# Eight key matmuls of a decoder kernel moved from a network's end phase into its four layers

## The chip, the cores and the metric

One core of one Trainium2 chip runs the whole program. The metric is the device time in microseconds (us) of one execution. The engines are PE (TensorE, matrix products and transposes), ACT (ScalarE), DVE (VectorE), POOL (GpSimd) and SP (SyncE, which only issues DMAs here).

## The reference, cut to what matters

Two decoder layers run on eight sequences (b = 0 to 7) of 128 tokens by 512 features, each sublayer followed by a residual sum and a layer norm. Two sublayers meet in the stretch of this case. The first is a small network of depth 4 on 64 channels:

```
h = x @ Win.T + bin
for each of 4 layers:
    y = silu(layernorm(h, ln1w, ln1b))
    y = sconv(y)                       # a long convolution, in the kernel a scan
    h = h + y * scl
    y = layernorm(h, ln2w, ln2b)
    y = silu(y @ W1.T + b1) @ W2.T + b2
    h = h + y
out = layernorm(h, lnlw, lnlb) @ Wout.T + bout
x = layernorm(x + out)
```

The second is cross attention: queries from x, keys and values from the context, which is an input and so is known from the start:

```
q = x @ Wq + bq            # 32 heads of 128
k = ctx @ Wk + bk          # 8 heads of 128
v = ctx @ Wv + bv
x = layernorm(x + softmax(q k^T / sqrt(128)) v @ Wo + bo)
```

## The kernel before, in words

Each engine has its own instruction list in program order; semaphores join them. The order around the change is written out by hand.

**The keys.** K transposed is made for 8 heads (g) and 2 halves of the batch (four sequences, 512 tokens), so in 16 banks' worth of result (n = 0 to 15), each a sum over four blocks of 128 features. This gives 64 matmuls of 128x512 in plain float32, called pieces here; the trace records each as two matmuls (L842). Pieces of even n go to PSUM bank 3, of odd n to bank 7. After the fourth piece of an n, ACT copies the bank to SBUF with the bias (`keys` on ACT, recorded as L1035, "arena<-psum,prm 128x512"). Since the context is ready early, the pieces can stand anywhere before the first scores, and they are used as filling: the table `KV_PLAN` says how many pieces stand at which numbered place, and `kv_pieces(at)` turns it into a range. PE and ACT call `keys(at)` at the same places.

**The places.** 0 is ahead of the layers. In layer l the numbers are 1 + 8l + c: c = 0 and 1 after the transposes of the first norm (L852, one group per half h), c = 2 and 3 after the product that follows the scan (L858), c = 4 and 5 after the transposes of the second norm (L865), c = 6 and 7 after the second product of the feed-forward part (L878, which follows L871). `KV_LAST` = 33 is behind the last norm's transposes (L886), 34 behind the first four output products of the network (`network_out`, L896), and 35 to 38 behind the queries j = 0 to 3 of the first head group.

**The end phase of the network.** PE does `last_turn` (L886), keys, `network_out(0..3)` (L896), keys, `turn_half(0, 0)` and `turn_half(0, 1)` (L914, the transposes of the normed x), `network_out(4, 5)`, `turn_half(0, 2)`, `network_out(6, 7)`, `turn_half(0, 3)`. DVE's list runs beside it: for b = 0 to 3 the sum and statistics (`ln_a`, L1652 to L1656) and the normed x (`ln_b`, L1660), then `x_rest` (L2029, the rest of the split of x into two float32r parts); ACT makes the first part (`turned_half`, "x_split<-psum"). `turn_half(0, 2)` waits for the first `x_rest`, `turn_half(0, 3)` for the second.

**The queries.** `query(0, j)` is 12 matmuls in float32r (L547 to L549) into bank 0. It waits for `q_sb`, that is until ACT has copied the query before out of bank 0 (`query_out`). After `query(0, 3)` the loop over the steps s begins with the scores of step 0 (L982), which wait for the fourth query's copy, for all 16 key copies (`kv_sb`) and for the values.

The lines that put a piece into its place, on PE:

```
        def kv_pieces(at):
            before = sum(c for a, c in KV_PLAN.items() if a < at)
            return range(before, before + KV_PLAN.get(at, 0))
...
            for j in range(GQ):
                query(0, j)
                keys(KV_LAST + 2 + j)
            pe.wait_ge(S.x_sum, lnc(3, B - 1))
            pe.wait_ge(S.kv_sb, 2 * NKV)
```

Of the kernel before, what the change touches and what calls it, by code (L numbers as in the profile page):

```python
# [57 lines left out]

KVL = 8
KV_LAST = 1 + 4 * KVL  # L60
KV_PLAN = {0: 6, KV_LAST: 2, KV_LAST + 1: 4}
for _l in range(4):
    KV_PLAN.update({1 + _l * KVL + 1: 4, 1 + _l * KVL + 2: 2, 1 + _l * KVL + 3: 3, 1 + _l * KVL + 7: 3})
    KV_PLAN[KV_LAST + 2 + _l] = 1
OUT_BANK = (2, 6, 5, 4)
LORA_BANK = (0, 1, 2, 4)
FFN_BANK = (2, 4, 3)
# [78 lines left out]
def decoder_kernel(nc, xT, xtok, ctxT, ctxtok, par, rows, four, win, wx, wdt, wout, qw, sc, ze,  # L146
# [3 lines left out]
    with ExitStack() as ctx:  # L150
# [252 lines left out]
# [5 lines that stand above are left out]
# [1773 lines left out]
```

## Time and profile before

| | us |
|---|---|
| median of 3 runs | 1334.72 |
| lowest and highest of them | 1332.58, 1335.19 |
| the profiled execution | 1333.96 |
| its span, first to last instruction | 1332.2 |
| PE busy in it | 1236.0 (93%) |
| DVE, ACT, POOL busy | 968.5, 748.2, 674.8 |

The span is what the rows of the trace cover; 1.76 us of the profiled execution lie outside it. The stretch of this case is short: the layers run from 674.7 to 777 us of the span, the end phase from there to the first scores at 811.4 us. Layers follow each other every 24.36 us (the first norm's transposes, L852, start at 728.59 us in layer 2 and at 752.95 us in layer 3). In a timeline row the first number is the start, the second the duration of the row's instructions together; a bracket at the end gives the idle time of the engine just ahead and what ended it.

### The profile page before, as it was taken

To read this page: it belongs to the slowest core of one execution; us is meant where nothing else is said; L and a number is where in the kernel's file an instruction comes from. 1 tells how busy PE (TensorE), PEld (TensorE's weight loads), DVE (VectorE), ACT (ScalarE), POOL (GpSimd) and SP (SyncE) were. 2 spreads that over 40 slices of the span, in tenths; PEclk is the share of its full clock that TensorE was granted. 3 is DMA by queue.
4 is the path that set the end of the run, shared out by engine and by line. 5 is a ranking of instruction groups with operands and counts; after the bars stand their busy time and mean duration, and the time that the engine had idled before them with its cause. 6 is when DMAs were issued, how large, how long until landed. Compare 5 with 4: busy or idle time off the path is not lost.

```text
span 1332.2 us, 18653 instructions
## 1 busy us (share of the span) xinstructions
PE 1236.0 (93%) x6464; PEld 925.4 (69%) x6464; DVE 968.5 (73%) x1770; ACT 748.2 (56%) x1478; POOL 674.8 (51%) x535
## 2 busy tenths in 40 slices
PE   6997899999998988998998999999998999999995
PEld 5876677767777764444565547888887888888874
DVE  4785798999999997898657766655554675666676
ACT  5479898989998983332133235544544445444441
POOL 4128988888988870222842126443433543333331
PEclk9999899999999999999999999999998999999999
DMA  6003200122220015002300103222221221111110
GB/s 182 12 26 139 75 25 25 35 93 88 88 72 1 1 56 136 16 9 85 144 9 16 40 24 103 80 73 71 68 75 48 80 79 65 63 64 64 48 48 32
DMA packets 37213, 81.92 MB, mean 61 GB/s; under 512 B 3808, under 2 KB 8160, under 8 KB 35200
## 3 DMA queue, kind: packets, MB, share of 16 engines
q1 hardware_dynamic: 37120, 80.72, 18.5%
q8 instruction: 53, 0.87, 0.3%
q14 instruction: 40, 0.33, 0.1%
HBM read 74.35 MB, written 6.36 MB: 61 GB/s over the span
## 4 chain that ended last, share of the span: by engine, by line
PE 68%; DVE 19%; ACT 6%; issue 5%; POOL 1%; DMA 1%; SPq 1%; DVEq 0%; POOLq 0%; ACTq 0%
PE psum L547 10%; PE psum L549 10%; PE psum L548 10%; PE psum L622 7%; PE psum L636 6%; PE psum L982 4%; DVE arena L1747 4%; PE psum L660 3%; PE psum L647 3%; ACT arena L1035 3%; PE psum L747 2%; PE psum L1001 2%; PE psum L731 1%; DVE lnst L1654 1%; PE psum L871 1%
## 5 line engine op out<-in xcount | busy, mean ns | idle before, releaser
L1471 POOL TENSOR_TENSOR arena<-arena 128x1024 f32<-128x1024 f32 x128 | 300.4, 2370 | 42.7 <-DVE arena L1747 42.5
L1407 POOL TENSOR_TENSOR w_split<-arena,w_split 128x512 fp32r<-128x512 f32 x128 | 168.1, 1333 | 280.3 <-ACT w_split L1035 280.3
L1747 DVE TENSOR_TENSOR_SCAN arena<-psum,arena 128x512 f32<-128x512 f32 x256 | 292.3, 1204 | 15.2 <-ACT psum L1035 15.2
L622 PEld LDWEIGHTS psum<-prm,arena 128*128 128x128 f32 x1024 | 118.7, 142 | 110.3 <-issue 61.8
L1035 ACT ACTIVATE psum<-arena,amat 128x508 f32<-128x508 f32 x256 | 173.3, 709 | 30.4 <-DVE arena L1747 29.4
L622 PE MATMUL psum<-prm,arena 128*128 128x128 f32 x1024 | 148.9, 280 | 38.4 <-DVE arena L1747 34.7
L1035 ACT ACTIVATE arena<-psum,ssmC 128x256 f32<-128x256 f32 x448 | 177.5, 484 | 10.8 <-PE psum L622 10.7
L1035 ACT ACTIVATE arena<-arena 128x512 f32<-128x512 f32 (+2 forms) x86 | 62.8, 734 | 210.1 <-DVE arena L2043 209.1
L1035 ACT ACTIVATE arena<-psum,prm 128x512 f32<-128x512 f32 (+1 forms) x130 | 91.1, 708 | 148.6 <-PE psum L549 70.0
L636 PE MATMUL psum<-prm,arena 128*128 128x128 f32 x1024 | 134.1, 273 | 0.1
L636 PEld LDWEIGHTS psum<-prm,arena 128*128 128x128 f32 x1024 | 117.0, 141 | 0.4 <-ACT arena L1035 0.3
L547 PE MATMUL psum<-x_split,w_split 128*128 128x512 f32 x256 | 106.3, 415 | 2.9 <-DVE x_split L2029 2.8
L1035 ACT ACTIVATE arena<-psum 128x512 f32<-128x512 f32 (+4 forms) x108 | 57.8, 563 | 82.7 <-PE psum L739 33.3
L1391 POOL TENSOR_TENSOR lnrs<-lnve,halfneg 128x1 f32<-128x1 f32 x48 | 28.4, 591 | 143.3 <-DVE lnve L1656 143.3
L549 PE MATMUL psum<-x_split,w_split 128*128 128x512 f32 x256 | 100.9, 394 | 0.0
L548 PE MATMUL psum<-x_split,w_split 128*128 128x512 f32 x256 | 100.8, 394 | 0.0
L547 PE MATMUL psum<-w_split,o_split 128*128 128x512 f32 x256 | 100.7, 394 | 0.0
L549 PE MATMUL psum<-w_split,o_split 128*128 128x512 f32 x256 | 100.1, 391 | 0.0
L548 PE MATMUL psum<-w_split,o_split 128*128 128x512 f32 x256 | 99.6, 389 | 0.0
L2040 DVE TENSOR_REDUCE amax<-psum 128x4 f32<-128x512 f32 x64 | 44.1, 688 | 52.4 <-PE psum L982 52.4
L2059 DVE TENSOR_TENSOR ssmT<-psum,p_split 128x512 fp32r<-128x512 f32 x64 | 44.2, 691 | 51.5 <-ACT p_split L1035 51.4
L2049 DVE TENSOR_REDUCE asum<-arena 128x4 f32<-128x512 f32 x64 | 43.9, 686 | 44.0 <-ACT arena L1035 44.0
(230 smaller groups left out, 2544.0 us busy)
## 6 DMA issues: line engine op xcount, KB each, us to landing
arena<-wq SPq DMA_DIRECT2D x64, 256.0 KB, 2.6
arena<-wo SPq DMA_DIRECT2D x64, 256.0 KB, 2.8
arena<-bc_scratch SPq DMA_DIRECT2D x8, 1024.0 KB, 5.2
arena<-win SPq DMA_DIRECT2D x16, 256.0 KB, 2.7
v_keep<-row SPq DMA_DIRECT2D x16, 256.0 KB, 2.1
arena<-v_keep SPq DMA_DIRECT2D x1, 4096.0 KB, 12.8
arena<-xT SPq DMA_DIRECT2D x8, 256.0 KB, 5.5
x_tok<-wv SPq DMA_DIRECT2D x1, 2048.0 KB, 7.7
```

The costliest lines, as they stand in the source:

```text
L547: mm(o, l[0], r[0], start=start, stop=False)
L548: mm(o, l[0], r[1], start=False, stop=False)
L549: return mm(o, l[1], r[0], start=False, stop=stop)
L622: last = nc.tensor.transpose(hT[:, c, b % 2, e, :], hst[:, (2 * k + e) % 4, b * L:(b + 1) * L], ident)
L636: last = mm(bank[6 + e][:, b * L:(b + 1) * L], hTs[:, k % 2, b, e, :], ident, start=(n == 0 and b == 0), stop=(n == NS - 1 and b == HB - 1 ...
L982: last = mm(bank[1][:, j * P:(j + 1) * P], qT[:, v % 2, j, b * L:(b + 1) * L], KT[:, v % NKV, gb * L:(gb + 1) * L], start=True, stop=True)
L1035: return nc.scalar.activation(o, i, f, **k)
L1407: gp.tensor_tensor(out_, whole, hi.bitcast(F32), ALU.subtract).then_inc(done, 1)
L1471: gp.tensor_tensor(bu[:, i % 4, :, :], dtu[:, (2 * j + e) % 4, :].unsqueeze(1).to_broadcast([P, NG, HT]), Brep[:, q * NG:(q + 1) * NG, :], ...
L1747: v.tensor_tensor_scan(hst[:, i % 4, :], decay_bank(i), bu[:, (k // NG * 2 + e) % 4, k % NG, :], 0.0, ALU.mult, ALU.add).then_inc(S.scan_d ...
L2040: link(v.tensor_reduce(amax[:, :], ps, AX.X, ALU.max))
L2059: v.tensor_tensor(p_lo[:, r % 2, :], bank[2][:, :], p_hi[:, r % 2, :].bitcast(F32), ALU.subtract).then_inc(S.p_rest, 1)
```

## The change

Only the table changes. Each layer gets four pieces instead of three at c = 3 and at c = 7, so eight more in all; the four pieces at place 34 and the four at places 35 to 38 are gone, the two at 33 stay.

```diff
-KV_PLAN = {0: 6, KV_LAST: 2, KV_LAST + 1: 4}
+KV_PLAN = {0: 6, KV_LAST: 2}
...
-    KV_PLAN.update({1 + _l * KVL + 1: 4, 1 + _l * KVL + 2: 2, 1 + _l * KVL + 3: 3, 1 + _l * KVL + 7: 3})
-    KV_PLAN[KV_LAST + 2 + _l] = 1
+    KV_PLAN.update({1 + _l * KVL + 1: 4, 1 + _l * KVL + 2: 2, 1 + _l * KVL + 3: 4, 1 + _l * KVL + 7: 4})
```

The file is one line shorter, so every line number behind the table is one lower after it. On PE, from the product behind the scan of layer 2 to the transposes of layer 3's first norm, the order before is this (here a piece counts once):

```order
L858 MATMUL psum<-arena 128x64 x4
L842 MATMUL psum<-arena 128x512 x3
L865 MATMUL psum<-prm,arena 64x128 x8
L871 MATMUL psum<-arena 128x512 x4
L878 MATMUL psum<-arena 128x64 x16
L842 MATMUL psum<-arena 128x512 x3
L852 MATMUL psum<-prm,arena 128x128 x8
```

and after the change:

```order
L857 MATMUL psum<-arena 128x64 x4
L841 MATMUL psum<-arena 128x512 x4
L864 MATMUL psum<-prm,arena 64x128 x8
L870 MATMUL psum<-arena 128x512 x4
L877 MATMUL psum<-arena 128x64 x16
L841 MATMUL psum<-arena 128x512 x4
L851 MATMUL psum<-prm,arena 128x128 x8
```

One piece has come in ahead of each norm's transposes; the other three layers read alike.

On PE in the end phase, from the last norm's transposes to the first half's last transposes, before:

```order
L886 MATMUL psum<-prm,arena 64x128 x8
L842 MATMUL psum<-arena 128x512 x2
L896 MATMUL psum<-dwout_sb,arena 128x512 x4
L842 MATMUL psum<-arena 128x512 x4
L914 MATMUL psum<-prm,x_tok 128x128 x8
L896 MATMUL psum<-dwout_sb,arena 128x512 x2
L914 MATMUL psum<-prm,x_tok 128x128 x4
L896 MATMUL psum<-dwout_sb,arena 128x512 x2
L914 MATMUL psum<-prm,x_tok 128x128 x4
```

and after:

```order
L885 MATMUL psum<-prm,arena 64x128 x8
L841 MATMUL psum<-arena 128x512 x2
L895 MATMUL psum<-dwout_sb,arena 128x512 x4
L913 MATMUL psum<-prm,x_tok 128x128 x8
L895 MATMUL psum<-dwout_sb,arena 128x512 x2
L913 MATMUL psum<-prm,x_tok 128x128 x4
L895 MATMUL psum<-dwout_sb,arena 128x512 x2
L913 MATMUL psum<-prm,x_tok 128x128 x4
```

The four pieces between the output products and the transposes are gone; behind these rows the one piece after each of the four queries is gone too.

The copies on ACT move with the fourth pieces. Before, each layer had one at c = 1, c = 2 and c = 7, and two followed in the queries' stretch or just ahead of it. After, layers 0 and 2 have one at c = 1, 2, 3 and 7, layers 1 and 3 one at c = 1, 3 and 7, and the last stands at place 33. In layers 0 and 2 the one at c = 3 stands on ACT directly ahead of the two copies of the second norm (L1034 after the change, d_tr), as ACT's list of layer 2 shows, before:

```order
L1035 ACTIVATE arena<-psum,prm 128x512 [waits kv_ps] x2
L1035 ACTIVATE arena<-psum,prm 64x512 [waits d_tr] x2
L1035 ACTIVATE arena<-psum,prm 128x512 [waits d_f1]
```

and after:

```order
L1034 ACTIVATE arena<-psum,prm 128x512 [waits kv_ps] x3
L1034 ACTIVATE arena<-psum,prm 64x512 [waits d_tr] x2
L1034 ACTIVATE arena<-psum,prm 128x512 [waits d_f1]
```

A third key copy now stands ahead of the second norm's copies.

## Rows read from the trace of the kernel before

**Rows 1.** The page: shares of the span by engine in the chain that ended last.
```profile
PE 68%; DVE 19%; ACT 6%; issue 5%; POOL 1%; DMA 1%; SPq 1%; DVEq 0%; POOLq 0%; ACTq 0%
```

**Rows 2.** Timeline of PE in layer 2: start, duration, line, shape, count, idle before.
```profile
729.95 3.60 PE L842 MATMUL psum<-arena 128*128 128x512 f32 x8
733.38 1.00 PE L858 MATMUL psum<-arena 128*128 128x64 f32 x8
...
736.89 2.79 PE L842 MATMUL psum<-arena 128*128 128x512 f32 x6
740.36 0.63 PE L865 MATMUL psum<-prm,arena 128*64 128x128 f32 x4 [0.68 <-DVE arena L1974]
741.23 0.63 PE L865 MATMUL psum<-prm,arena 128*64 128x128 f32 x4 [0.24 <-DVE arena L1974]
741.86 3.70 PE L871 MATMUL psum<-arena 64*128 64x512 f32 x8
...
749.11 2.79 PE L842 MATMUL psum<-arena 128*128 128x512 f32 x6
752.95 0.66 PE L852 MATMUL psum<-prm,arena 128*128 128x128 f32 x4 [1.05 <-DVE arena L1974]
```

**Rows 3.** Timeline of ACT at layer 2's second norm.
```profile
741.03 0.78 ACT L1035 ACTIVATE arena<-psum,prm 64x512 f32<-64x512 f32 x1 [4.15 <-PE psum L865]
```

**Rows 4.** Waits, 676 to 780 us: who for whom, us in total, times, longest.
```profile
PEld psum L871 <- ACT arena L1035: 1.1, 4, 0.3
```

**Rows 5.** Timeline of PE in the end phase.
```profile
783.73 3.70 PE L842 MATMUL psum<-arena 128*128 128x512 f32 x8
787.27 1.04 PE L914 MATMUL psum<-prm,x_tok 128*128 128x128 f32 x8
788.24 1.98 PE L896 MATMUL psum<-dwout_sb,arena 64*128 64x512 f32 x4
790.40 0.63 PE L914 MATMUL psum<-prm,x_tok 128*128 128x128 f32 x4 [0.19 <-DVE x_split L2029]
...
794.94 0.50 PE L547 MATMUL psum<-x_split,w_split 128*128 128x512 f32 x1 [1.41 <-DVE x_split L2029]
...
798.83 0.47 PE L547 MATMUL psum<-x_split,w_split 128*128 128x512 f32 x1
...
806.51 0.47 PE L547 MATMUL psum<-x_split,w_split 128*128 128x512 f32 x1
...
811.40 1.13 PE L982 MATMUL psum<-arena 128*128 128x128 f32 x8 [1.06 <-ACT arena L1035]
```

**Rows 6.** Timeline of DVE in the end phase.
```profile
781.26 0.69 DVE L1652 TENSOR_TENSOR x_tok<-x_tok,psum 128x512 f32<-128x512 f32 x1 [3.49 <-PE psum L896]
...
784.75 0.54 DVE L1660 TENSOR_SCALAR x_tok<-x_tok,lnmv,lnrs 128x512 f32<-128x512 f32 x1
...
786.94 0.54 DVE L1660 TENSOR_SCALAR x_tok<-x_tok,lnmv,lnrs 128x512 f32<-128x512 f32 x1
...
789.57 0.68 DVE L2029 TENSOR_TENSOR x_split<-psum,x_split 128x512 fp32r<-128x512 f32 x1
```

**Rows 7.** Timeline of ACT between the queries.
```profile
798.00 0.69 ACT L1035 ACTIVATE arena<-psum,prm 128x512 f32<-128x512 f32 x1 [3.84 <-PE psum L549]
...
810.62 0.68 ACT L1035 ACTIVATE arena<-psum,prm 128x512 f32<-128x512 f32 x1
```

**Rows 8.** Stretches: length, busy us and count of PE, PEld, DVE, ACT, POOL, PEclk, DMA.
```profile
609.60:613.00 3.40, 0.69 (x5) 0.52 (x5) 3.30 (x7) 1.99 (x4) 0.00 (x0) 1.00 0.00 0
613.00:616.40 3.40, 3.40 (x4) 1.33 (x5) 1.60 (x4) 0.00 (x0) 1.48 (x7) 0.50 0.00 0
1011.60:1015.70 4.10, 1.50 (x13) 1.12 (x12) 2.64 (x4) 1.63 (x4) 0.00 (x0) 1.00 0.21 64
1015.90:1022.50 6.60, 5.19 (x15) 3.82 (x14) 2.15 (x4) 0.96 (x2) 0.00 (x0) 0.50 0.00 0
783.80:788.20 4.40, 4.40 (x17) 2.31 (x16) 4.19 (x11) 0.73 (x2) 1.56 (x2) 1.00 0.00 0
```

## The prediction

> **What bounds the kernel now.** I read the page first: of the span's 1332.2 us the chain of work that ended last is two thirds PE, one fifth DVE [rows 1]. That is an average. The change lives in 137 us of it, so the timelines of that stretch decide, engine beside engine.
>
> In a layer the chain changes hands. PE runs without a gap from the second norm's transposes through both feed-forward products into the key pieces, and then waits for DVE's norm. The timeline of PE in layer 2 shows the two waits at which the change puts work [rows 2]: the pieces from 736.89 end 0.68 us before the transposes L865 may start, and those from 749.11 end 1.05 us before L852. Both were ended by DVE (L1974), which had no earlier moment. So PE is not late there, it is filled up to a remainder. The other layers repeat the pattern with their period of 24.36 us.
>
> In the end phase the bound is DVE. It starts its first sum at 781.26 and reaches the first `x_rest` (L2029) at 789.57 [rows 6], and in 783.80 to 788.20 it is busy 4.19 of 4.40 us [rows 8]. Its whole list in that time hangs on nothing that PE does late. PE's third group of transposes (L914 at 790.40) waits for that `x_rest` and starts 0.15 us after its end at 790.25 [rows 5, 6]. Then come two output products, the fourth transposes, ACT, DVE and the first query at 794.94.
>
> From the first query on, PE and ACT alternate: a query, its copy out of bank 0 by ACT, and beside the copy one key piece.
>
> **What the move costs in the layers.** One piece at c = 3. Four pieces take 733.38 - 729.95 = 3.43 us from their start to the next instruction's start [rows 2], so from 736.89 they would reach 740.32. L865 starts at 740.36. It fits, by 0.04 us. Cost 0, at the least; at the most, if all four layers miss by a little, 0.1 each.
>
> One piece at c = 7: 749.11 + 3.43 = 752.54, and L852 starts at 752.95 [rows 2]. It fits by 0.4 us. The cover is PE's wait for DVE. Without this cover a piece costs its own 0.86 us (3.43 / 4), and eight of them 6.9 us.
>
> The copies on ACT. They number 16 as before, but in layers 0 and 2 one now stands at c = 3, directly ahead of the copy of the second norm. Its bank is full when the fourth piece ends, at 740.32 + 0.16 (rows of four pieces last 3.60 and free PE after 3.43) = 740.48. Each key copy takes 0.69 us [rows 7], so ACT is free at about 741.1 to 741.2. Before, ACT began the norm's copy at 741.03 [rows 3]. The first product behind it, L871, does wait for this copy: its weight load waited four times for ACT, 0.3 us at the longest [rows 4], and 741.03 + 0.78 = 741.81 meets its start at 741.86 [rows 2, 3]. So the delay of 0.1 to 0.2 us goes straight onto the path, since PE is gapless behind it. In two layers that is 0.15 x 2 = 0.3 us; from 0 to 0.5. The copy at c = 7 of those layers begins about 752.7 and is over at 753.4, while L852's result comes at 752.95 + 0.66 = 753.6: nothing.
>
> The weights of the keys. SP loads head g's weights once the piece count frees the buffer. The pieces now come earlier, but so does the release, as both follow the same counter, and a load lies at least one group of layers' places (over 10 us) ahead of its use. Nothing is queued on SP behind it that could start earlier, because the query weights wait for the last layer's product. Cost 0.
>
> **What it brings in the end phase.** The four pieces at place 34 lasted from 783.73 to 787.27, 3.54 us of PE [rows 5]. Without them the first transposes could start when x of b = 0 is normed, 784.75 + 0.54 = 785.29, and the second when b = 1 is, at 787.48 [rows 6]. That is 2.0 and 0.3 us sooner. But what follows needs `x_rest`, and DVE reaches it in its own order at 789.57 whatever ACT and PE did. The third transposes still start at 790.40 and the first query at 794.94. Of 3.54 us nothing is won; PE stands idle instead. From both sides: 0, or if DVE had waited for ACT, which its busy time excludes, some tenths. I take 0.
>
> The four pieces behind the queries. A query and its piece take 798.83 - 794.94 = 3.89 us [rows 5]. Without the piece the next query waits for ACT: from a query's start to ACT's start 798.00 - 794.94 = 3.06, the copy 0.69 [rows 7], and from a copy's end to PE's start 811.40 - (810.62 + 0.68) = 0.10 [rows 5, 7]. Together 3.85. The piece was hidden behind the copy: 0.04 us won on the first, between 0 and 0.1 on each of the next two. Say 0.1 for the three.
>
> The last piece is different. Before, the scores at 811.40 waited for ACT's copy of the last keys, begun at 810.62 after the last piece [rows 5, 7]. After, that copy is long done, and the scores need only the last query's copy. The last query began at 806.51 [rows 5]; 806.51 + 3.85 = 810.36, less the 0.1 above 810.26. Won: 811.40 - 810.26 = 1.1 us with that 0.1. Its bounds are 0.9 (a first matmul slower after a gap) and 1.4.
>
> **The sum.** -1.1 + 0.3 = -0.8 us against the profiled execution's 1333.96, which lies 0.76 under the median of 1334.72. The same steps taken from the median: 1334.72 - 0.8 = 1333.9 us. The bounds of the terms give -1.4 to 0. Behind 811.40 all engines' lists shift together, and from there PE is the bound, so I carry the gain to the end unchanged.
>
> **The rivals.** First, the clock, and with it a slower kernel. After the change PE between 783.8 and 788.2 has only two short groups of transposes, about 1.1 us together, with idle times of some 1.5 us ahead of each (785.3 - 783.8, and 787.5 less 785.9); before, it was busy throughout [rows 8]. The trace shows what emptier stretches do: in 609.60 to 613.00 PE was busy 0.69 us, and then it ran at 1.2 GHz (granted 0.50) for 3.4 us; after 1011.60 to 1015.70 with 1.50 us busy came 6.6 us at 1.2 GHz [rows 8]. If the clock falls at about 787.1, the output products at 788.24 (1.98 us for four records [rows 5]) are at half speed. With 3.4 us of it, the third transposes start some 0.8 us later; with 6.6 us, both pairs of products (1.7 us each more, less the part that meets the full clock again) and the transposes are hit, about 2.3 us. Net of the 0.8: 1333.9 + 0.8 = 1334.7 to 1333.9 + 2.3 = 1336.2 us. If the low clock reaches the first query too, its 3.06 us [rows 5, 7] become up to 6, and the time 1339. It decides as soon as the loss passes 0.8. For it: the new gap is nearly as empty as the two that fell. Against: it is two gaps with work between, not one of 2.6, and the queries' new gaps of 0.8 us are no more than those that the layers have at full clock. A quarter.
>
> The Trainium skill (TensorE: Matmul & The Clock Gate, Part 4: PE-mode transpose) says that transposes don't count as work for the clock in the way matmuls do. By that rule all of 783.8 to 788.2 is one idle stretch, and the fall would be near certain, for a time of about 1336.2 in place of 1333.9. Both stretches of [rows 8] that ended in a fall held transposes and the rule fits them, but they had little work of any kind, so they don't show it.
>
> Second, the layers miss their turn. The fit at c = 3 is 0.04 us. If the pieces or the copies push L865, L871 and DVE by 0.3 us in every layer, the gain of 1.1 is given back: 1334.8, and at 0.5 each 1335.6. Against it: the second half's transposes have another 0.24 us of wait [rows 2], which takes up a late first half. One in eight.
>
> Third, a larger gain: the removed PE time counts in full, 3.54 + 4 x 1.0 = 7.5 us (a piece among queries is 3.89 less the query's 3.06 - 0.16 = 2.9), less the 0.3, so 1327.5. This needs DVE and ACT to be faster than their rows. One in twenty.
>
> **How the numbers follow.** My forecast, 1333.9 with 1333.1 to 1334.7 as its own range, has 0.57; the clock 0.25; the layers 0.13; the larger gain 0.05. Each comes with the spread of a median of a few runs (before: 1332.58 to 1335.19). The range 1332.0 to 1336.3 leaves out the larger gain and the clock's worst, and some of the spread. About 0.2%, 2.7 us, is what a measurement of this kernel can tell from no change. Faster by more (under 1332.0): the larger gain and a little of the forecast's spread, 0.09. Slower by more (over 1337.4): the clock's worst and the spread above its 1336.2, 0.07. Within: 0.84.
>
> **What would show it.** Right: in the timeline of PE the first query starts within 0.3 us of the distance it had from the first DVE sum (794.94 - 781.26 = 13.7); queries 3.8 us apart with 0.8 us idle "<-ACT" between; scores 15.3 us after the first query instead of 16.5; the layers' period 24.36 in layers 1 and 3, up to 24.6 in 0 and 2; no idle ahead of the first L865 and about 0.2 ahead of L852. Wrong: a granted clock under 1 between 785 and 800 us, products of L896 at double length, or layer periods above 24.7.

## The result and the profile after

The changed kernel takes 1342.62 us (median of 6 executions, 1339.75 to 1350.37), the kernel before 1334.45 us (6 executions, 1332.58 to 1335.19): a ratio of 1.0067 with an interval of 1.004 to 1.0095. It is slower. Measured once more, 12 executions beside 35 of the kernel before (e12 below), it is 1341.66 against 1335.92 us, ratio 1.0035, interval 1.0014 to 1.0056. (The ratios here and below are not the quotients of the two medians and can differ from them by 0.1%.) Single executions lie up to 8 us (changed) and 11 us (before) over their medians, with a lower mean clock; hence the wide intervals.

The page of the changed kernel, its span and its row of granted clocks (40 slices of 33.5 us, in tenths of 2.4 GHz):

```profile
span 1339.9 us, 18653 instructions
PEclk8999899999999999999999979999998999999999
```

The slice at 7, the 24th (770 to 804 us), is the end phase. In the kernel before it stood at full clock.

The timeline of PE in layer 2 answers to [rows 2] (all line numbers behind the table are one lower):

```profile
738.67 3.65 PE L841 MATMUL psum<-arena 128*128 128x512 f32 x8
742.16 0.61 PE L864 MATMUL psum<-prm,arena 128*64 128x128 f32 x4
743.00 0.63 PE L864 MATMUL psum<-prm,arena 128*64 128x128 f32 x4 [0.24 <-DVE arena L1973]
743.76 3.70 PE L870 MATMUL psum<-arena 64*128 64x512 f32 x8
...
751.01 3.65 PE L841 MATMUL psum<-arena 128*128 128x512 f32 x8
754.85 0.66 PE L851 MATMUL psum<-prm,arena 128*128 128x128 f32 x4 [0.18 <-DVE arena L1973]
```

Both groups of pieces have grown by one, the wait ahead of the first L864 is gone, and that ahead of L851 has shrunk from 1.05 to 0.18 us. From the start of the first L864 to that of L870 it is 1.60 us; before it was 1.50. It is 1.60 us in layer 0 too, and 1.47 us in layers 1 and 3, where the key copy at this place follows the second piece and not the fourth. So the 0.1 us is the copy on ACT, which now stands ahead of the norm's; the waits of the layers, 1.1 us before [rows 4], have grown with it.

```profile
PEld psum L870 <- ACT arena L1034: 1.3, 4, 0.4
```

The end phase on PE, as [rows 5]:

```profile
782.02 3.70 PE L895 MATMUL psum<-dwout_sb,arena 64*128 64x512 f32 x8
787.27 0.66 PE L913 MATMUL psum<-prm,x_tok 128*128 128x128 f32 x4 [1.54 <-DVE x_tok L1659]
789.45 1.12 PE L913 MATMUL psum<-prm,x_tok 128*128 128x128 f32 x4 [1.52 <-DVE x_tok L1659]
790.49 3.77 PE L895 MATMUL psum<-dwout_sb,arena 64*128 64x512 f32 x4
794.20 1.11 PE L913 MATMUL psum<-prm,x_tok 128*128 128x128 f32 x4
795.24 3.78 PE L895 MATMUL psum<-dwout_sb,arena 64*128 64x512 f32 x4
798.95 1.11 PE L913 MATMUL psum<-prm,x_tok 128*128 128x128 f32 x4
...
801.48 0.79 PE L546 MATMUL psum<-x_split,w_split 128*128 128x512 f32 x1 [1.41 <-DVE x_split L2028]
...
807.33 0.47 PE L546 MATMUL psum<-x_split,w_split 128*128 128x512 f32 x1 [0.87 <-ACT arena L1034]
...
818.85 1.13 PE L981 MATMUL psum<-arena 128*128 128x128 f32 x8 [0.87 <-ACT arena L1034]
```

Two waits of 1.5 us stand where the four pieces were. From the second transposes on, PE's work takes nearly twice its time: four transposes 1.1 instead of 0.6 us, two output products 3.8 instead of 2.0. The two stretches show why, with the granted clock third from the end:

```profile
785.60:788.80 3.20, 0.78 (x5) 0.42 (x4) 2.99 (x9) 0.60 (x1) 0.82 (x2) 0.98 0.00 0
788.80:805.80 17.00, 14.94 (x30) 7.92 (x31) 9.88 (x22) 1.79 (x3) 2.09 (x3) 0.50 0.00 0
```

TensorE was busy 0.78 of 3.20 us and then ran at 1.2 GHz for 17.0 us. And DVE's list, which continues [rows 6], now has long waits. The third and fourth `x_rest` before:

```profile
791.69 0.69 DVE L2029 TENSOR_TENSOR x_split<-psum,x_split 128x512 fp32r<-128x512 f32 x1 [0.38 <-ACT x_split L1035]
794.19 0.69 DVE L2029 TENSOR_TENSOR x_split<-psum,x_split 128x512 fp32r<-128x512 f32 x1 [1.81 <-ACT x_split L1035]
```

and the first, third and fourth after:

```profile
791.49 0.68 DVE L2028 TENSOR_TENSOR x_split<-psum,x_split 128x512 fp32r<-128x512 f32 x1
...
795.98 0.69 DVE L2028 TENSOR_TENSOR x_split<-psum,x_split 128x512 fp32r<-128x512 f32 x1 [2.75 <-ACT x_split L1034]
800.73 0.69 DVE L2028 TENSOR_TENSOR x_split<-psum,x_split 128x512 fp32r<-128x512 f32 x1 [4.06 <-ACT x_split L1034]
```

The first `x_rest` still comes where DVE's own list puts it, 8.31 us after its first sum (783.18; before 789.57 - 781.26 = 8.31). The third and fourth wait for ACT, which waits for PE's transposes. These waits were 0.38 and 1.81 us and are 2.75 and 4.06 us; together they have grown by 4.62 us, and that is by how much more the first query is late.

Where the 7.7 us between the two spans went, by the starts of the same instructions:

| stretch | before | after | difference |
|---|---|---|---|
| to the first key pieces | 674.68 | 676.33 | +1.65 |
| layers, to the first output product | 105.42 | 105.69 | +0.27 |
| from there to the first query | 14.84 | 19.46 | +4.62 |
| first query to the second | 3.89 | 5.85 | +1.96 |
| second query to the scores | 12.57 | 11.52 | -1.05 |
| scores to the end of the span | 520.8 | 521.05 | +0.25 |

The first row is not the change's. No instruction moved ahead of 676 us; there this execution had 3.4 us at 1.2 GHz near 471 us (granted clock 0.89 over 465 to 480 us, 1.00 in the one of before). The 0.25 us of the last row I leave open. The four rows between add up to 5.8 us, which is the change's part; the medians of e12 lie 5.7 us apart.

### The profile page after: what moved, and what is told of

Read it like the earlier page. It is cut to its first block, busy times and chain, and to the rows that moved or that the text cites. A ratio compares the mean times of both kernels' runs of the same rounds, so it can differ in the third digit from the quotient of the medians.

```text
span 1339.9 us, 18653 instructions
## 1 busy us (share of the span) xinstructions
PE 1243.6 (93%) x6464; PEld 929.6 (69%) x6464; DVE 968.9 (72%) x1770; ACT 748.6 (56%) x1478; POOL 675.4 (50%) x535
## 4 chain that ended last, share of the span: by engine, by line
PE 68%; DVE 18%; ACT 6%; issue 4%; POOL 1%; DMA 1%; SPq 1%; DVEq 0%; POOLq 0%; ACTq 0%
PE psum L546 10%; PE psum L548 10%; PE psum L547 10%; PE psum L621 7%; PE psum L635 6%; PE psum L981 4%; DVE arena L1746 4%; PE psum L659 3%; ACT arena L1034 3%; PE psum L646 3%; PE psum L746 2%; PE psum L841 2%; PE psum L1000 2%; DVE lnst L1653 1%; PE psum L870 1%
## 5 line engine op out<-in xcount | busy, mean ns | idle before, releaser
L1034 ACT ACTIVATE psum<-arena,amat 128x508 f32<-128x508 f32 x256 | 173.1, 708 | 29.8 <-DVE arena L1746 28.9
L1034 ACT ACTIVATE arena<-psum,ssmC 128x256 f32<-128x256 f32 x448 | 177.8, 484 | 11.6 <-PE psum L621 11.6
L1034 ACT ACTIVATE arena<-arena 128x512 f32<-128x512 f32 (+2 forms) x86 | 62.8, 734 | 209.9 <-DVE arena L2042 208.9
L1034 ACT ACTIVATE arena<-psum,prm 128x512 f32<-128x512 f32 (+1 forms) x130 | 91.0, 709 | 144.7 <-PE psum L548 73.6
L1034 ACT ACTIVATE arena<-psum 128x512 f32<-128x512 f32 (+4 forms) x108 | 57.8, 563 | 82.7 <-PE psum L738 33.3
```

Source lines behind the costliest of these rows:

```text
L1034: return nc.scalar.activation(o, i, f, **k)
```

## The experiments

My theory after the result: emptying the place ahead of the transposes lets TensorE's clock fall, and all of the loss is what the end phase then takes longer. Rivals: the new waits between the queries do it or share in it; the pieces in the layers cost more than they seem to. For each kernel the table gives the time from the first output product (L895) to the first scores (L981) in its profile, besides the whole. The time to the scores leaves out what differs elsewhere between executions. The kernel before ran beside each group.

| kernel | product to scores, us | low clock there, us | median (executions), us | median of before, us | ratio (interval) |
|---|---|---|---|---|---|
| before | 31.30 | none | | | |
| changed | 36.83 | 788.8 to 805.8 | 1342.62 (6) | 1334.45 | 1.0067 (1.004, 1.0095) |
| e1 | 30.24 | none | 1334.94 (12) | 1336.34 | 0.9999 (0.9974, 1.0024) |
| e2 | 38.44 | 793.0 to 813.5 | 1343.08 (7) | 1336.34 | 1.0044 (1.003, 1.0058) |
| e3 | 30.27 | none | 1335.91 (12) | 1336.34 | 1.0003 (0.9984, 1.0023) |
| e4 | 30.25 | none | 1335.29 (11) | 1336.34 | 0.9992 (0.9983, 1.0001) |
| e5 | 30.35 | none | 1335.10 (12) | 1335.88 | 0.9987 (0.9965, 1.0009) |
| e6 | 30.27 | none | 1335.49 (12) | 1335.88 | 0.9989 (0.9963, 1.0015) |
| e7 | 28.53 | none | 1332.84 (12) | 1335.88 | 0.9976 (0.9951, 1.0002) |
| e8 | 30.76 | 793.2 to 796.6 | 1333.83 (12) | 1335.88 | 0.9975 (0.9953, 0.9996) |
| e9 | 30.28 | none | 1336.07 (12) | 1335.92 | 1.0007 (0.9982, 1.0033) |
| e10 | 30.49 | 787.2 to 790.6 | 1335.57 (9) | 1335.92 | 1.0004 (0.9978, 1.0031) |
| e11 | 28.07 | none | 1332.84 (12) | 1335.92 | 0.9989 (0.9963, 1.0015) |
| e12 | 36.97 | 793.0 to 810.1 | 1341.66 (12) | 1335.92 | 1.0035 (1.0014, 1.0056) |

### e1 and e2: each half of the change alone

```diff
# e1: the pieces behind the queries moved, those ahead of the transposes kept
+KV_PLAN = {0: 6, KV_LAST: 2, KV_LAST + 1: 4}
...
+    KV_PLAN.update({1 + _l * KVL + 1: 4, 1 + _l * KVL + 2: 2, 1 + _l * KVL + 3: 3, 1 + _l * KVL + 7: 4})
# e2: the pieces ahead of the transposes moved, those behind the queries kept
+KV_PLAN = {0: 6, KV_LAST: 2}
...
+    KV_PLAN.update({1 + _l * KVL + 1: 4, 1 + _l * KVL + 2: 2, 1 + _l * KVL + 3: 3, 1 + _l * KVL + 7: 4})
+    KV_PLAN[KV_LAST + 2 + _l] = 1
```

> Only the four pieces behind the queries are moved (into the layers, one more at c = 7 of each); the four between the network's output products and the transposes stay. Theory A (the emptied stretch before the transposes lets the clock fall, and that is the whole loss): the clock stays at 2.4 GHz from 675 to 1012 us, queries 3.84 us apart with about 0.87 us idle, scores about 1.1 us sooner: 0.5 to 1.5 us faster than before. Theory B (the new waits between the queries are part of what keeps the clock low): a low clock between 795 and 812 us and a loss of 2 us or more.

> Only the four pieces ahead of the transposes are moved (one more at c = 7 of each layer); those behind the queries stay. Theory A: the clock falls near 788 us as in the changed kernel, the first query starts 18 to 20 us after the first output product instead of 14.8, 5 to 8 us slower than before. Theory B, in which the queries' waits are needed too: a short fall at most, 0 to 2 us slower.

PE's timeline of e1 from the transposes on:

```profile
795.50 0.50 PE L546 MATMUL psum<-x_split,w_split 128*128 128x512 f32 x1 [1.41 <-DVE x_split L2028]
799.38 0.47 PE L546 MATMUL psum<-x_split,w_split 128*128 128x512 f32 x1 [0.87 <-ACT arena L1034]
...
810.90 1.13 PE L981 MATMUL psum<-arena 128*128 128x128 f32 x8 [0.87 <-ACT arena L1034]
```

The waits between the queries are there, 0.87 us each, the queries are 3.88 and 3.84 us apart as with pieces between them, and the scores come 30.24 us after the first product, 1.06 sooner than before. The stretch from 785 to 800 us has full clock:

```profile
785.00:800.00 15.00, 12.53 (x46) 6.82 (x46) 12.31 (x28) 4.07 (x7) 3.03 (x5) 1.00 0.00 0
```

e2 has no such waits and falls, for 20.5 us:

```profile
788.15 3.70 PE L896 MATMUL psum<-dwout_sb,arena 64*128 64x512 f32 x8
793.39 1.12 PE L914 MATMUL psum<-prm,x_tok 128*128 128x128 f32 x4 [1.54 <-DVE x_tok L1660]
...
796.62 3.78 PE L896 MATMUL psum<-dwout_sb,arena 64*128 64x512 f32 x4
...
807.61 0.80 PE L547 MATMUL psum<-x_split,w_split 128*128 128x512 f32 x1 [1.41 <-DVE x_split L2029]
...
826.59 1.13 PE L982 MATMUL psum<-arena 128*128 128x128 f32 x8 [1.06 <-ACT arena L1035]
```

```profile
790.00:795.00 5.00, 2.97 (x9) 1.25 (x7) 4.69 (x14) 0.46 (x1) 1.33 (x2) 0.80 0.18 52
```

So the queries' waits are out as a cause, and the loss belongs to the four pieces ahead of the transposes. The gain of 1.06 us shows in the trace alone: over whole executions e1 can't be told from before.

e2 shows one thing more. Its first group of transposes already runs at half speed (1.12 us), and a granted clock of 0.80 over 790 to 795 us puts the fall at 793.0, only 1.1 us into the first wait and directly behind 3.7 us of output products without a rest. So the fall does not need both waits. Nor does the share of busy time order the cases by itself: in the 3.40 us ahead of this fall the products filled 2.25, more than in the stretches of [rows 8] that ended in one. They were products over 64 rows. Whether that is the reason, or at what moment the wait came, no run here settles.

### e3, e4 and e9: the empty place filled again, with three kinds of work

In the changed kernel, work that nobody reads is put where the four pieces were. It goes to PSUM bank 3, behind the last copy out of it.

```diff
# e3: four products over 128 rows
+            def fill(n):
+                for i in range(n):
+                    mm(bank[3][:, :], wk_sb[:, 0, 0:P], ctxT_sb[:, 1, i % KD, :], start=True, stop=True)
...
-            keys(KV_LAST + 1)
+            pe.wait_ge(S.kv_sb, 15)
+            fill(4)
# e4: in place of fill(4), 32 transposes
+            for i in range(32):
+                nc.tensor.transpose(bank[3][:, i % 4 * P:(i % 4 + 1) * P], ctxT_sb[:, 0, i // 4 % KD, i % 4 * P:(i % 4 + 1) * P], ident)
# e9: fill(4) with products over 64 rows
+                    mm(bank[3][:, :], wk_sb[0:DIM, 0, 0:P], ctxT_sb[0:DIM, 1, i % KD, :], start=True, stop=True)
```

> The changed kernel with four needless 128x512 float32 matmuls (their result is never read) in the place that the four moved pieces left ahead of the transposes. Theory A: no fall there, 0.5 to 1.5 us faster than before, some 8 us faster than the changed kernel. A rival in which the loss comes from moved work in the layers or from another order of the copies: it stays 5 to 8 us slower.

> The changed kernel with 32 needless 128x128 transposes (about 3.5 us of the engine) in the same place. If any work of TensorE keeps its clock: as with the matmuls, 0.5 to 1.5 us faster than before. If transposes don't count as work, as the Trainium skill says (TensorE: Matmul & The Clock Gate, Part 4: PE-mode transpose): the clock falls and it is 5 to 8 us slower than before.

> As e3, four needless products ahead of the transposes in the changed kernel, but over 64 rows in place of 128, of the same length in time. If the rows a product fills matter to the clock, and 64 are too few to keep it: it falls, and the time is 5 to 8 us over that of before. If they keep it like 128 rows and like transposes: as e3, within 1 us of before. In between (some executions fall) the theory that only the share of busy time counts is out as well.

The filling and its stretch in e4, and then in e9:

```profile
783.85 3.72 PE L906 MATMUL psum<-prm,arena 128*128 128x128 f32 x32
783.80:788.20 4.40, 4.40 (x41) 4.35 (x40) 4.18 (x11) 0.16 (x1) 1.59 (x3) 1.00 0.00 0
```

```profile
784.44 3.59 PE L906 MATMUL psum<-arena 64*128 64x512 f32 x8
780.90:789.00 8.10, 8.10 (x26) 3.79 (x25) 6.59 (x16) 1.03 (x2) 3.13 (x4) 1.00 0.10 32
```

All three keep the clock, and product to scores is 30.27, 30.25 and 30.28 us: the same to 0.03. With the place filled, the whole loss is gone and the scores' gain of 1.0 us is there. Over whole executions all three are level with the kernel before; the 0.5 to 1.5 us that I had expected to see there are too small for it. The pieces in the layers are the changed kernel's in all three, so they don't carry the loss. The rule of the Trainium skill (TensorE: Matmul & The Clock Gate, Part 4: PE-mode transpose) that transposes don't count as work is not borne out here for keeping the clock: in e4 the engine did nothing but float32 transposes for 3.7 us, and more of them behind, with a granted clock of 1.00, and none of its 11 executions took over 1337.24 us. Whether transposes alone can lift a clock that is down, no run here shows. Products over 64 rows, 7.1 us of them without a rest in e9, kept the clock too: the first half of e9's expectation fell.

### e5: the layers' part by itself

As e3, and one needless product behind each query too, so that TensorE does all that it did before and eight pieces more.

```diff
+            fill(4)
...
                 query(0, j)
-                keys(KV_LAST + 2 + j)
+                fill(1)
```

> The changed kernel with needless 128x512 float32 matmuls in all eight places that the moved pieces left (four ahead of the transposes, one behind each query). TensorE so does what it did before, and eight pieces more in the layers: this times the layers' part alone. If the layers take the pieces in their waits: 0 to 0.5 us slower than before, and the layers of the trace 0.3 us longer in all. If they don't: 2 us slower or more. Against the kernel with four needless matmuls (e3) it gives back the 1 us that the freed scores brought.

The queries and the scores:

```profile
797.22 0.50 PE L546 MATMUL psum<-x_split,w_split 128*128 128x512 f32 x1 [1.41 <-DVE x_split L2034]
...
812.73 1.13 PE L987 MATMUL psum<-arena 128*128 128x128 f32 x8
```

The layers are as in the changed kernel (100.41 us from the transposes of the first norm of layer 0 to the first output product, 100.43 there), and the whole is 1335.10 us against 1335.88, interval 0.9965 to 1.0009: no cost that can be measured. My last expectation missed. I wrote that the products behind the queries would give back the 1 us. They don't (30.35 us, against 30.27): what had delayed the scores was not the last piece on PE but ACT's copy of the last keys, and a needless product has none.

### e6: half of the filling

```diff
+KV_PLAN = {0: 6, KV_LAST: 2, KV_LAST + 1: 2}
...
+    KV_PLAN.update({1 + _l * KVL + 1: 4, 1 + _l * KVL + 2: 2, 1 + _l * KVL + 3: 3 + _l % 2, 1 + _l * KVL + 7: 4})
```

> The changed kernel, but two of the four pieces stay ahead of the transposes (two layers take one piece less at c = 3). TensorE's empty stretch there shrinks from two waits of 1.5 us to about one. If the clock falls as soon as any such wait is there: 5 to 8 us slower than before. If half the filling is enough: 0.5 to 1.5 us faster. A mixture over the executions (some near the one time, some near the other) would say that it hangs on where in the chip's own rhythm the stretch lies.

```profile
785.41 1.98 PE L841 MATMUL psum<-arena 128*128 128x512 f32 x4
787.23 0.60 PE L913 MATMUL psum<-prm,x_tok 128*128 128x128 f32 x4
789.20 0.66 PE L913 MATMUL psum<-prm,x_tok 128*128 128x128 f32 x4 [1.37 <-DVE x_tok L1659]
```

One wait of 1.37 us is left, and the clock stays up. One of its 12 executions took 1346.64 us, the other eleven at most 1337.67; the kernel before had such single ones as well (up to 1346.96), so a mixture doesn't show. Two pieces were enough in this one profile.

### e8, e10 and e12: why it stayed low so long

In the changed kernel TensorE never rested from 789.45 to 800.06 us, and still ran at 1.2 GHz to 805.8. Most of that time it did the output products, which use 64 of the array's 128 rows. In e8 they are taken over 128 rows; the added rows of the weights are zero, so the result is the same.

```diff
+        dwout_all = dwout_rows[:, :]
...
+            link(gp.memset(dwout_rows[DIM:P, :], 0.0))
...
-                mm(bank[OUT_BANK[b % HB]][:, :], dys[0:DIM, b // HB, (b % HB) * L:(b % HB + 1) * L], dwout_sb,
+                mm(bank[OUT_BANK[b % HB]][:, :], dys[:, b // HB, (b % HB) * L:(b % HB + 1) * L], dwout_all,
```

> The changed kernel, with the network's output products (L895) over 128 rows in place of 64; the added rows of the weights are zero, so the result is the same, and so is a product's duration. In the changed kernel the clock stayed at 1.2 GHz through 10.6 us in which TensorE never rested, most of it in these products, and came back only in the first query. If half-filled products don't lift the clock: with full rows it comes back before the first query, at 792 to 799 us in place of 805.8, and the loss shrinks from 8 to 2 to 5 us. If rows don't matter: as the changed kernel, low to the first query.

> The kernel of e8 once more, for a second profile: its 12 executions had a median of 1333.8 us and the profiled one 1339.4, the slowest. If full rows in the output products keep the clock in most executions: a profile with no fall between 785 and 800 us, the scores 30 to 30.5 us after the first output product, and 1332 to 1334.5 us. If it falls in all and only comes back sooner: a fall of 3.4 us near 790 again and 1336 us or more.

> The changed kernel itself, on the chip and beside the executions of before that the other three use. If it falls in every execution: every time 5 us or more over the median of before, and a profile with a low clock for 13 us or more from about 789 us.

PE's timeline of e8:

```profile
793.21 1.11 PE L914 MATMUL psum<-prm,x_tok 128*128 128x128 f32 x4 [1.52 <-DVE x_tok L1661]
794.12 3.12 PE L896 MATMUL psum<-dwout_sb,arena 128*128 128x512 f32 x4
797.08 0.60 PE L914 MATMUL psum<-prm,x_tok 128*128 128x128 f32 x4
797.51 1.88 PE L896 MATMUL psum<-dwout_sb,arena 128*128 128x512 f32 x4
```

The fall is there, but the clock is back after 3.4 us, within the first pair of products. The second pair takes 1.88 us, and product to scores is 30.76 us instead of 36.83. Of the loss, of which I had expected 2 to 5 us to stay, nothing is left: e8 is even below the kernel before by its interval, though e10, the same kernel, is level with it. e10's profile gives the same picture with other times; its stretch at the low clock:

```profile
787.20:790.60 3.40, 2.98 (x7) 1.89 (x8) 3.30 (x8) 0.60 (x1) 1.54 (x2) 0.52 0.00 0
```

Of the two outcomes written down for e10 the profile decides for the second: the full rows don't prevent the fall, they end it. (Its time, 1335.57 us, lies just under the 1336 that I had put to it.) e12, the changed kernel again, has its 17.1 us at 1.2 GHz:

```profile
793.00:810.20 17.20, 15.24 (x31) 8.13 (x32) 10.04 (x23) 1.79 (x3) 2.08 (x3) 0.50 0.00 0
```

Its 12 executions range from 1338.90 to 1349.07; the lowest is 3.0 us over the median of before, not 5 as I had written, though none is below it. So two things make the loss: the empty place, in which the clock fell in all five profiles that have it (changed, e2, e8, e10, e12), and the 64-row products behind it, through which it stayed down until the queries. The second rests on one edit, the rows, with two profiles on one side and three on the other.

### e7 and e11: a version with a shorter end phase

e7 starts from e1 and lets the third and fourth transposes write banks of their own, 7 and 3, ahead of the last two output products, so that they need no `x_rest`; they wait for the last two key copies instead, and ACT and DVE read the new banks (these waits and reads are not in the lines shown). e11 has the full rows of e8 as well.

```diff
-            turn_half(0, 2, 0)
+            turn_half(0, 2, 7)
+            turn_half(0, 3, 3)
             for b in range(HB + 2, B):
                 network_out(b)
-            turn_half(0, 3, 1)
```

> The pieces as in e1 (four kept ahead of the transposes, none between the queries), and the third and fourth transposes write PSUM banks of their own (7 and 3, in which the keys are done) in place of 0 and 1, ahead of the last two output products; so they no longer wait for DVE's rests. If DVE's list is the bound of this stretch, as I said, it now runs on without its waits for ACT (0.4 and 1.8 us): the first query 1.3 to 2.2 us sooner, and 2 to 3.5 us faster than before in all. If something else binds there: as e1.

> e7 (four pieces kept ahead of the transposes, none between the queries, own banks for the third and fourth transposes) with the output products over 128 rows. If both gains stand beside each other: the scores 28.5 us after the first output product as in e7, and 2 to 4 us faster than before. The rows should add nothing where the clock doesn't fall.

PE and then DVE in e7:

```profile
792.30 1.27 PE L915 MATMUL psum<-prm,x_tok 128*128 128x128 f32 x8
793.50 1.98 PE L895 MATMUL psum<-dwout_sb,arena 64*128 64x512 f32 x4
795.41 0.50 PE L546 MATMUL psum<-x_split,w_split 128*128 128x512 f32 x1
```

```profile
793.62 1.30 DVE L2030 TENSOR_TENSOR x_split<-psum,x_split 128x512 fp32r<-128x512 f32 x2 [0.17 <-ACT x_split L1036]
```

DVE waits 0.17 us for ACT where it had waited 0.4 and 1.8, and the first query comes without a wait, 13.15 us after the first output product instead of 14.84. With the scores' gain, product to scores is 28.53 us, 2.8 less than before. e11 has 28.07, and there I missed: I had written that the rows add nothing where the clock holds. Four output products over 128 rows take PE 3.44 us to the next instruction, over 64 rows 3.62, and in e7 PE is what the first query follows. The medians are 3.0 and 3.1 us under those of before, but both intervals hold 1: the gain is shown in one profile each and not settled over executions.

## Why the prediction was wrong, point by point

**The layers: right.** I had 0.3 us in all, from ACT's copy in layers 0 and 2, and nothing for PE. The trace has 0.27 us. L870 starts 1.60 us after the first L864 in layers 0 and 2, 0.10 more than before, and not later than before in layers 1 and 3. The pieces fit at c = 3 with nothing over and leave 0.18 us ahead of L851, where I had 0.04 and about 0.2. e5 finds no cost over executions.

**The end phase: the mechanism of the forecast was right, while the clock held.** The first `x_rest` comes 8.31 us after DVE's first sum in both kernels; nothing was won by emptying PE. In e3, e4 and e9, which hold the clock, the stretch is what the forecast said: 1.0 us less, all of it the last copy of the keys. But DVE is the bound only as far as the first `x_rest`. Behind it it waited, before the change too, 0.38 and 1.81 us for ACT and so for PE's transposes: from 790.4 us on PE's speed counts directly, and there the low clock struck.

**The queries: right.** They follow each other 3.84 us apart with 0.87 us of wait for ACT, and from the second one to the scores it is 1.05 us less; I had 1.1.

**The clock: here it failed.** The sum has no term for it; it stands only in the first rival, and two steps of that were wrong. The first was its chance. I gave it a quarter and argued that two gaps with work between are less than one of 2.6 us. My rows said nothing for that: one stretch of them that ended in a fall had 0.69 us busy in 3.40, and the new one, which I had called "nearly as empty", has 0.78 in 3.20. In all five profiles with this place empty the clock fell, in e2 within the first of the two gaps. The second was its length, and so its price. I took 3.4 or 6.6 us from [rows 8]; it was 17.0 us. The cost was 4.62 us to the first query and 1.96 us in it, together 6.6, where I had 0.8 to 2.3 and, beyond it, a first query doubled as an afterthought, for 1339 us at the most. I had priced the low clock as if the work behind the gap would lift it. e8 and e10 show what I had missed. The work behind the gap is 64-row products; made over 128 rows, the clock comes back after 3.4 us and 6.1 to 6.3 of the 6.6 us are gone. A fall of 3.4 us, which I had priced at 0.8 us, costs at least 0.5 in e8 and 0.2 in e10 (30.76 and 30.49 against e3's 30.27); the full rows gain something of their own, 0.46 us in e11 against e7, so the price may be up to that much higher.

**A slip in the sum.** The bounds of the terms, -1.4 to 0, give 1333.3 to 1334.7 from the median; the forecast's own range says 1333.1. It changes nothing here.

**The rule of the Trainium skill** (TensorE: Matmul & The Clock Gate, Part 4: PE-mode transpose) pointed to the outcome that came, but its reason is not the one at work: transposes alone kept the clock in e4, and in e2 it fell before any transpose had run in the place.

## What to carry to other kernels

Before work is taken out of a place in which the engine waits anyway, read how empty the place becomes and what stands ahead of it and behind it: here the filling cost nothing, and without it TensorE ran at 1.2 GHz for 17 us. Price a fall of the clock by the work that follows, not by the shortest fall in the trace. A chain that is bound by another engine can be shortened where that engine waits (e7: banks of their own for two transposes), and not by giving the idle engine less to do.

## What the runs showed of the hardware that I had not expected

- Products over 64 rows kept a full clock (e9, 3.6 us of filling behind 3.7 us of output products, granted 1.00), yet TensorE stayed at 1.2 GHz through 10.6 us of such products and transposes without a rest. With the same products over 128 rows it was back at 2.4 GHz after 3.4 us, in two profiles.
- Thirty-two transposes in a row, 3.7 us, kept the clock as well as products did.
- The zeros in the added rows did not matter to this: half of what the 128-row products multiply is zero, and the clock came back all the same (e8, e10).
- One wait was enough: in e2 the clock fell 1.1 us after the end of 3.7 us of 64-row products without a rest.
